# A dense mixture in a two-layer decoder: both rounds in one 16-entry program, with the gate behind the first product

## What is computed

```python
xt = x.reshape(-1, H)
res = xt
for j in range(C):                                   # C = 2
    gate = xt @ Wg[j] + bg[j]                        # 8 logits
    _, ids = jax.lax.top_k(gate, K)                  # K = 6
    in_top = jax.nn.one_hot(ids, NE, dtype=gate.dtype).sum(-2) > 0
    w = jax.nn.softmax(jnp.where(in_top, gate, -jnp.inf), axis=-1)
    h = jnp.einsum('th,nhe->nte', xt, Wup) + bup[:, None, :]
    h = jax.nn.silu(jnp.einsum('nte,nef->ntf', h, Wsw) + bsw[:, None, :]) * h
    eo = jnp.einsum('nte,neh->nth', h, Wdn) + bdn[:, None, :]
    out = jnp.einsum('nth,tn->th', eo, w[:, :N])     # 6 routed experts
    ...
    out = out + sh.reshape(-1, S * E) @ Wsd + bsd    # 2 shared ones, weight 1
    xt = res + out
```

## Time and profile before

| | us |
|---|---|
| median of 3 runs (lowest, highest) | 2240.31 (2236.24, 2246.9) |
| span of the profiled execution | 2238.0 |
| mean granted clock of PE in it | 0.931 of 2.4 GHz |
| busy: PE, DVE, ACT, POOL | 1962.5, 1424.5, 1058.8, 634.7 |

### The profile page before, as it was taken

One profiled execution on the slowest core, in us unless ns is written; L12 is line 12 of the kernel. 1 busy time (PEld: TensorE's weight loads), 2 busy tenths in 40 slices (PEclk: granted clock), 3 DMA queues, 4 the chain that ended last, 5 costly groups with the idle time before them and its releaser, 6 DMA issues. The chain is left out here.

```text
span 2238.0 us, 36241 instructions
## 1 busy us (share of the span) xinstructions
PE 1962.5 (88%) x12872; PEld 1195.9 (53%) x12872; DVE 1424.5 (64%) x2696; ACT 1058.8 (47%) x2118; POOL 634.7 (28%) x542
## 2 busy tenths in 40 slices
PE   6888877978999799996999999997588896899998
PEld 4555544446777477772544545454155563355553
DVE  5666575366775667766756758477699956545334
ACT  4666634132333323341645637264499993344332
POOL 3555500022332323320110101011667770132320
PEclk9999997988999889998999999999599967999999
DMA  4000003111110201104001010000910003476533
GB/s 138 25 25 1 1 1 118 38 56 41 47 47 0 72 24 47 47 0 137 20 20 51 27 38 19 0 1 1 216 32 2 2 2 132 146 193 175 136 71 90
DMA packets 96111, 125.46 MB, mean 56 GB/s; under 512 B 9296, under 2 KB 52560, under 8 KB 95968
## 3 DMA queue, kind: packets, MB, share of 16 engines
q1 hardware_dynamic: 89248, 107.79, 15.9%
q0 software_dynamic: 6720, 15.73, 3.7%
HBM read 101.67 MB, written 18.61 MB: 54 GB/s over the span
## 5 line engine op out<-in xcount | busy, mean ns | idle before, releaser
L1170 POOL TENSOR_TENSOR wl<-stage,wh 128x512 fp32r<-128x512 f32 x80 | 117.3, 1498 | 395.9 <-DVE wh L1161 395.9
L1429 POOL TENSOR_TENSOR Zl<-z,Zh 128x512 f16<-128x512 f32 x32 | 51.2, 1599 | 494.1 <-ACT Zh L1590 494.1
L77 PE MATMUL PS<-XTh,wh 128*128 128x512 f16 x416 | 161.0, 387 | 19.8 <-ACT t L2013 19.0
L1270 ACT ACTIVATE h<-PS,bup 128x512 f32<-128x512 f32 x64 | 44.2, 690 | 278.4 <-PE PS L79 278.4
L2482 POOL TENSOR_TENSOR PTl<-P,PTh 128x512 f16<-128x512 f32 (+2 forms) x160 | 149.9, 945 | 66.6 <-ACT PTh L2637 63.9
L78 PE MATMUL PS<-XTl,wh 128*128 128x512 f16 x416 | 160.5, 386 | 0.0
L79 PE MATMUL PS<-XTh,wl 128*128 128x512 f16 x416 | 160.2, 385 | 0.0
L2636 ACT ACTIVATE P<-PS 128x512 f32<-128x512 f32 (+3 forms) x256 | 143.8, 562 | 17.0 <-PE PS L2573 15.3
L2637 ACT ACTIVATE PTh<-PS 128x512 f16<-128x512 f32 (+3 forms) x256 | 145.4, 568 | 0.0
L2651 DVE TENSOR_REDUCE M<-PS 128x1 f32<-128x640 f32 (+3 forms) x128 | 127.0, 1012 | 4.1 <-PE PS L2555 4.1
L2573 PE MATMUL PS<-QS,KS 98*128 98x512 f16 (+3 forms) x256 | 99.8, 391 | 28.1 <-ACT PTh L2637 15.3
(11 more groups left out here) (377 smaller groups left out, 6032.3 us busy)
## 6 DMA issues: line engine op xcount, KB each, us to landing
stage<-in_ffn_W SPq DMA_DIRECT2D x18, 1024.0 KB
stage<-in_ffn_Wg SPq DMA_DIRECT2D x9, 1024.0 KB
stage<-in_ffn_Wup SPq DMA_DIRECT2D x16, 512.0 KB, 3.9
stage<-in_ffn_Wdn SPq DMA_DIRECT2D x16, 512.0 KB, 3.6
wq<-in_attn_wq SPq DMA_DIRECT2D x4, 1024.0 KB, 5.6
C<-in_ctx SPq DMA_DIRECT2D x8, 512.0 KB, 9.0
stage<-in_ffn_Wsw SPq DMA_DIRECT2D x16, 256.0 KB, 3.6
stage<-in_attn_WV SPq DMA_DIRECT2D x16, 256.0 KB, 4.0
```

The lines of the kernel that those rows point to most:

```text
L77: pe.matmul(out, a[0], b[0], start=start, stop=False, skip_group_check=True)
L1170: nc.gpsimd.tensor_tensor(piece(wl[q], ch), piece(st, ch), plain(piece(wh[q], ch)), ALU.subtract).then_inc(w_lo, 1)
```

## The change

- `ExpertWeights` holds staging buffer and parts, shares the space of the cross attention's context, and lives across phases. Entry 0's weights are loaded and split inside the cross attention: its five CASTs stand on DVE between the normalisation of tile 6 and the output of tile 7, its low parts are made by POOL.
- `GateInput`: both gates are loaded and split in the load phase.
- `phase_ffn0` is one program of 16 entries n (two rounds), with no barrier between. Between the rounds, `middle` (a `Norm` without normalisation) turns Y into XR.
- PE's order: first product of 0, logits, then per n: second product of n, first product of n+1, third product of n. The order of ACT, DVE and POOL follows: `body` on DVE is `g` and `Gl` of n, `Hl` of n+1, adds of n, CASTs for n+2.
- The residual pass is gone: the add of entry 0 reads X in place of the output. For round 2, POOL doubles X in 8 operations at n = 7.
- The bias product is one more matmul per tile of the third product of entries 7 and 15: 72 stacked rows (high and low parts of W and biases). ACT copies the turned weights twice, DVE subtracts once.
- `choose` compares with one broadcast operation each (128x512) in place of sixteen of 128x64.

```diff
 PE
-            gate.logits(pe)
+            def body(n, q):
+                second(n, q)
+                up(n + 1, 1 - q, range(UP))
+                down(n, q)
+            up(0, 0, range(UP))
+            gate.logits(pe, 0)
             body(0, 0)
             with pe.Fori(0, NE // 2 - 1) as i:
                 body(2 * i + 1, 1)
                 body(2 * i + 2, 0)
-            body(NE - 1, 1)
+            second(NE - 1, 1)
+            down(NE - 1, 1)
+            pe.wait_ge(middle.xt_lo, QT)
+            up(NE, 0, (0,))
+            middle.turn(pe, NT - 2)
+            up(NE, 0, (1,))
+            middle.turn(pe, NT - 1)
+            pe.wait_ge(middle.xt_lo, NT)
+            up(NE, 0, (2, 3))
+            pe.wait_ge(added, NT * NE)
+            gate.logits(pe, 1)
+            body(NE, 0)
...
+            def down(n, q):
+                final = isinstance(n, int) and n % NE == NE - 1
...
+                if final:
+                    pe.wait_ge(wt_hi, 2 * (n // NE + 1))
+                    pe.wait_ge(wt_lo, n // NE + 1)
+                    pe.wait_ge(bd_lo, 1)
+                    pe.wait_ge(silu_done, UP * (n + 1))
...
+                    if final:
+                        last = pe.matmul(c.PS[:, 4 + t % 4, :], WT[:, t, :], bd[:], start=False, stop=True,
+                                         skip_group_check=True)
 ACT
+            def body(n, e):
+                silus(n, e)
+                for m in range(UP):
+                    h_part(*after(n, e), m)
 DVE
+            def body(n, e, q, dst, more=True):
+                g_parts(n)
+                for m in range(UP):
+                    h_part(n + 1, m)
+                for t in range(NT):
+                    add(n, e, t, dst)
+                if more:
+                    weights.split_hi(dve, n + 2, q)
+            for m in (0, 1):
+                h_part(0, m)
+            weights.split_hi(dve, 1, 1)
+            for m in (2, 3):
+                h_part(0, m)
+            gate.choose(dve, 0)
+            split_bias()
+            body(0, 0, 0, Y)
...
+            body(N - 3, NE - 3, 1, c.X)
+            body(N - 2, NE - 2, 0, c.X, False)
 POOL
+            def body(n, q, more):
+                for m in (0, 2):
+                    pool.wait_ge(g_hi, UP * n + m + 1)
+                    nc.gpsimd.tensor_tensor(at(Gl, m), g32[:, m, :], plain(at(Gh, m)), ALU.subtract).then_inc(g_lo, 1)
+                if isinstance(n, int) and n == NE - 1:
+                    for t in range(NT):
+                        nc.gpsimd.tensor_tensor(c.X[:, t, :], c.X[:, t, :], c.X[:, t, :], ALU.add).then_inc(doubled, 1)
                 if more:
+                    weights.split_lo(pool, n + 2, q)
 cross attention 0, DVE
             for t in range(NT - 1):
                 norm.normalize(dve, t)
+            weights.split_hi(dve, 0, 0)
             output(NT - 1)
```

More of the change, by code:

```diff
@@ L245, in _ @@
             route.load(sp)
+            for gate in c.gates:
+                gate.load(sp)
         @block.tensor
@@ L302, in __init__, with logits @@
         self.chosen = c.sem(ctx, "chosen")
[L304 to L313, removed]
+        self.links = 0
+    def logits(self, pe, r):
+        of = self.inputs[r]
+        pe.wait_ge(of.parts, 2)
         for b in range(B):
@@ L361, in choose @@
[L361 to L374, removed]
@@ L386, in choose @@
[L386 to L391, removed]
+        per_row = G[:].unsqueeze(3).broadcast_to([P, NT, n, n])
@@ L1082, in phase_ffn0 @@
+def phase_ffn0(c, W, weights, gates, Y, **end):
     nc = c.nc
@@ L1250, in _ @@
                 body(2 * i + 2, 0)
-            body(NE - 1, 1)
+            second(NE - 1, 1)
[10 more added lines that the diff above has]
+            body(NE, 0)
+            with pe.Fori(NE // 2, NE - 1) as i:
+                body(2 * i + 1, 1)
+                body(2 * i + 2, 0)
+            second(N - 1, 1)
+            down(N - 1, 1)
             norm.late(norm.pe_step, pe)
@@ new lines, in _ @@
+            split_bias()
+            body(0, 0, 0, Y)
+            with dve.Fori(0, NE // 2 - 1) as i:
+                body(2 * i + 1, 2 * i + 1, 1, Y)
+                body(2 * i + 2, 2 * i + 2, 0, Y)
+            g_parts(NE - 1)
+            for t in range(NT):
+                add(NE - 1, NE - 1, t, Y)
+                middle.dve_step(dve, t)
+            middle.late(middle.dve_step, dve)
+            weights.split_hi(dve, NE + 1, 1)
+            for m in range(UP):
+                h_part(NE, m)
@@ L1346, in _ @@
+            gate.choose(dve, 1)
+            body(NE, 0, 0, c.X)
+            with dve.Fori(0, NE // 2 - 2) as i:
+                body(2 * i + NE + 1, 2 * i + 1, 1, c.X)
+                body(2 * i + NE + 2, 2 * i + 2, 0, c.X)
+            body(N - 3, NE - 3, 1, c.X)
+            body(N - 2, NE - 2, 0, c.X, False)
+            g_parts(N - 1)
+            for t in range(NT):
+                add(N - 1, NE - 1, t, c.X)
+                norm.dve_step(dve, t)
             norm.late(norm.dve_step, dve)
@@ L2725, in decoder @@
         c.route = RouterInput(c, ctx, c.inp["gate1_w"], c.inp["gate1_b"], c.inp["gate1_sel"])
+        c.gates = [GateInput(c, ctx, c.inp[f"gate0_w{r}"], c.inp[f"gate0_b{r}"]) for r in range(2)]
         phase_load(c, c.route)
```

480 lines of the change are left out of this document (271 added, 209 removed).

## The result

The changed kernel takes 2245.47 us in the median of 20 runs (2241.32 to 2254.84), the kernel before 2239.45 (2234.61 to 2246.9): a ratio of 1.0032, with an interval from 1.0019 to 1.0044, that is 4 to 10 us slower, 7 in the middle. The forecast was 14.5 slower: the way was right and the size twice too large. The move is under the 0.5% that was set as the border of a change. The profiled execution has a span of 2242.1, against 2238.0.

A forecast was written before the change was run, and what follows sets the result against it. The prediction took PE, busy 88% of the span, and its waits to bound the kernel. Moved work -34.2, waits +28.9 and clock +19.8 gave +14.5 on the median 2240.31: 2254.8 us, range 2229 to 2272.

The forecast's parts named there:

- What bounds the kernel, and the chain: Time goes where PE waits; CASTs, g, Gh, then ACT's Hh free bank 0 about 14.4 us after a third product.
- The waits, +28.9: PE waits about 3.3 us in the middle of the first product in 12 bodies, 2.41 us more each.
- The clock, +19.8: Each of the twelve waits drops the clock to 1.2 GHz for 3.3 us, costing 1.65 each; bounds nothing and 3.3.
- the strict reading: In PE's twelve first-product waits: a wait that does not fill an idle window costs no clock, so zero.
- The start, -23.2 and +5.4: Cross attention's end to expert 1's second product: 23.2 us shorter, but expert 0's CASTs ahead of the last tile add 5.4.
- The join, -19.4: Between the rounds, second product of expert 7 to that of round 2's expert 1: 100.1 us becomes 80.7.
- The end, +2.1: Third product of entry 15 starts 8.65 instead of 6.55 us after its second product, for turned weights and bias product.
- +13.6: Forecast sum over four stretches: cross attention's end to entry 1, the two loops, the join, round 2's end.
- the first rival: The loops' waits come but the clock stays at 2.4 GHz: -5.3, 2235 us, range 2225 to 2246; chance 0.25.
- the load phase's 0.9: The gates' four loads and splits in the load phase put an estimated 0.9 us ahead of the first attention.
- The second: Rival: no wait arises in the first products, CASTs run near 0.416 us; 2194 us, faster; chance 0.08.
- The third: Rival: low clock behind the waits lasts twice as long, or the moved start brings less; 2275 us; chance 0.12.

The follow-up runs named there:

- filled kernel: Changed kernel plus nine extra PE products, results thrown away, inside the wait of each first product of entries 2 to 7 and 10 to 15: 2228.94 us, ratio 0.9950.
- Experiment 6: Changed kernel with entry 0's five CASTs spread ahead of the outputs of tiles 4, 5 and 6 of the cross attention: 2242.99 us, ratio 1.0014.
- experiment 3: Changed kernel with one of an entry's five CASTs moved behind the g of the next entry: 2211.31 us, ratio 0.9878.
- experiment 1: The filled kernel: changed kernel with nine unread PE products in each of the twelve first-product waits: 2228.94 us, ratio 0.9950.
- experiment 7: Changed kernel with all CASTs behind the g, entry 0's spread in the cross attention, W turned early in entries 0 and 8: 2174.25 us, ratio 0.9710.
- experiment 2: Changed kernel with two of an entry's five CASTs, and POOL's two subtractions, moved behind the g of the next entry: 2192.99 us, ratio 0.9789.

## Why the prediction was wrong

- **What bounds the kernel, and the chain: right.** The wait moved to ACT's `Hh` in the middle of the first product, in 12 entries, and each link came within 0.15 us of its price.
- **The waits, +28.9: right in kind, 27.3 measured.** The waits are 3.0 in the mean, not 3.3: in the entry shown PE gets there 0.1 later and bank 0 comes free 0.1 sooner.
- **The clock, +19.8: this is the step that failed.** "I price each of the twelve at half of 3.3 us" took it that every wait of some 3 us drops the clock, as all seven of the first attention did. Here 7 to 10 of 12 did. A drop cost 1.3 to 1.7, or 2.9 where the low stretch was twice as long, so the price of one, 1.65, was close to the mean (14.8 for nine is 1.64; 1.5 to 1.7 in three more executions); the number of drops was wrong. The filled kernel puts the term at 14.8 in the execution at hand, 1.23 a wait. The bounds, nothing and 3.3, held it. The Trainium skill ("TensorE: Matmul & The Clock Gate", "What's actually happening") has the low clock come after at least one idle window. By the strict reading that the prediction took from this, the term would have been zero; 14.8 were measured, so that reading did not hold here.
- **The start, -23.2 and +5.4: right together, -18.6 against -17.8.** Experiment 6 confirms the second term, 4.7.
- **The join, -19.4: right, -18.8.**
- **The end, +2.1: too large, 0.7.** The third product of entry 15 did start later, 8.75 behind its second, as priced (8.65). But it took time off a wait behind it: the wait for DVE's normalisation fell from 2.94 to 1.07. The prediction left this overlap out.
- **The sum.** Of the 8.2 between +13.6 and the profile's +5.4, 5.0 are the clock, 1.6 the waits (28.9 against 27.3), 1.4 the end, 0.8 the start and -0.6 the join. All but the join err to the same side, so the sum was too high by more than its largest error. The stretches outside the loops became 37 us shorter, and the loops' waits with the clock behind them gave all of it back, and a little more.
- **The rivals.** The changed kernel's time lies in the first rival's range by luck: its condition, a clock that stays up, did not hold. What it describes, waits at full clock, is the filled kernel: -5.3 by the sum, 0.9950 or -11 measured, with an interval from -15 to -7. By the four stretches of the table the filled kernel is at -8.9, where the sum without the load phase has -6.2; of this 2.7, 1.6 is the waits and 0.8 the start. The rest, some 2 us and the load phase's 0.9, was not placed. The second did not come: CASTs beside POOL took 5.07, as before. The third did not come as a whole, though up to two waits an execution did cost twice as much.

## What to carry to other kernels

When a program is reordered, look at what stands directly ahead of the first link of the new chain on each engine: work that lay in slack under the old order (here five CASTs) may sit ahead of it under the new one, and here rows of the old profile priced the new chain to 0.15 us. The waits of about 3 us on PE cost 1.0 to 1.5 us each on top of what they held up, in the mean of an execution; halving them (experiment 3) or putting work into them (experiment 1) took that part away. And a term that depends on the clock is better put into a sum as a share of occasions, with a range, than as a fixed price for each.

## What the runs showed of the hardware

- Waits of equal length had different outcomes. Of 48 waits of 2.87 to 3.14 in four executions, 34 were followed by a stretch at 0.50; of twelve waits of 1.44 to 1.70 in experiment 3, none was. The first two waits of round 2 (2.9 and 3.1) were never followed by one, the four behind them always. In round 1 the first wait (2.9) was followed by one in one execution of four. Waits of 2.1 went both ways: the clock was 0.50 behind the 2.14 ahead of entry 15's third product in the changed kernel, 1.00 behind the same wait in experiment 1, and 1.00 behind the 2.11 of experiment 7. Why one wait falls and its neighbour does not was not settled.
- Nine matmuls per wait whose results are thrown away made the kernel 0.8% faster (a ratio of 0.9950 against 1.0032).
- CASTs beside POOL's subtractions do not cost a fixed price each: five in a row took 5.07, three 2.19, two 0.75 (experiment 2, behind the `Gl`). POOL's first operation starts 0.5 behind the first CAST each time, so the first CAST (0.416 at the shortest) is over before it; that this is the reason is a reading of the rows, no run tested it. In experiment 2:

```profile
559.97 0.75 DVE L1138 CAST wh<-stage 128x512 fp32r<-128x512 f32 x2
560.64 3.48 DVE L1432 TENSOR_TENSOR Hl<-h,Hh 128x512 fp32r<-128x512 f32 x2
```

The two `Hl` behind those two CASTs then took 3.48, beside POOL's two subtractions, where one `Hl` in the changed kernel takes 0.68 to 0.69 with POOL idle: here the cost moved to what DVE did next beside POOL.
